# Bias rows by one bf16 matmul, and bent rows completed on VectorE, in a graph attention layer

## The reference

```
q = x @ Wq + bq;  k = x @ Wk + bk;  v = x @ Wv + bv       (8 heads of 16)
e = edge_attr @ We
alpha = sum(q[dst] * (k[src] + e)) / 4        per head
a = exp(alpha - max over dst);  attn = a / sum over dst of a
out = sum over dst of attn * (v[src] + e)
x_r = x @ Wskip + bskip
beta = sigmoid([out, x_r, out - x_r] @ Wbeta);  out = beta * x_r + (1 - beta) * out
out = layernorm(out) * ln_gamma + ln_beta
y = x + relu(out)
result = layernorm(x + y)                      (so the last norm sees 2 x + relu(...))
```

## Time and profile before

| | |
|---|---|
| median of 3 runs | 2780.67 us (2771.22 to 2795.91) |
| profiled execution, span | 2774.7 us |
| PE busy | 2009.6 us (72%), 11492 instructions |
| PEld busy | 1805.8 us (65%) |
| DVE busy | 1801.8 us (65%), 4040 instructions |
| ACT busy | 1140.6 us (41%) |
| POOL busy | 1497.6 us (54%), 1591 instructions |
| mean granted PE clock | 0.770 of full speed |

### The profile page before, as it was taken

How to read it: one execution, slowest core, us unless ns; L and a number is a source line. 1 busy time by engine, 2 the same in 40 slices (tenths; PEclk the granted TensorE clock), 3 DMA queues, 4 the chain that set the end, 5 groups by cost and what they waited for, 6 DMA issues and landing times.

```text
span 2774.7 us, 45026 instructions
## 1 busy us (share of the span) xinstructions
PE 2009.6 (72%) x11492; PEld 1805.8 (65%) x11492; DVE 1801.8 (65%) x4040; ACT 1140.6 (41%) x3750; POOL 1497.6 (54%) x1591
## 2 busy tenths in 40 slices
PE   7478888888776577667766767757687777778775
PEld 5467777777666566566665767656576667667664
DVE  7465565566666566566665667657676676777764
ACT  0133333344343344344443444434454454454455
POOL 0555555555556555565555555555555555555531
PEclk9677777777777777777777777778788777777786
DMA  8556666666655555555554655555565555555541
GB/s 308 185 165 184 176 184 183 178 180 180 172 167 167 158 159 167 154 174 165 167 167 143 176 163 167 175 149 165 164 176 167 170 176 168 169 172 180 169 123 39
DMA packets 298585, 468.47 MB, mean 169 GB/s; under 512 B 49862, under 2 KB 193034, under 8 KB 298230
## 3 DMA queue, kind: packets, MB, share of 16 engines
q1 hardware_dynamic: 222680, 259.30, 31.3%
q0 software_dynamic: 75648, 206.24, 26.2%
HBM read 414.62 MB, written 50.73 MB: 168 GB/s over the span
## 4 chain that ended last, share of the span: by engine, by line
PE 54%; issue 17%; another core or an unknown queue 13%; ACT 8%; DVE 3%; DMA 2%; ACTq 1%; POOL 0%; SPq 0%; POOLq 0%; DVEq 0%
PE sum_ps L928 18%; PE q_ps L825 12%; PE e_ps L812 10%; ACT dist_en L1046 3%; PE max_ps L841 2%; PE sum_ps L866 2%; PE sum_ps L865 2%; PE sum_ps L851 2%; PE max_ps L834 2%; PE sum_ps L850 2%; ACT hot_en L1055 1%; PE sum_ps L894 1%; PE sum_ps L895 1%; DMA xt_buf<-xT 1%
## 5 line engine op out<-in xcount | busy, mean ns | idle before, releaser
L706 POOL DMA_INDIRECT kv<-kv_tab,src_all x1568 | 1483.1, 946 | 1144.6 <-DVE kve L1373 683.8
L1373 DVE TENSOR_TENSOR kve<-kv,e_ps 128x1024 f32<-128x1024 f32 x392 | 462.2, 1218 | 756.0 <-issue 626.2
L928 PE MATMUL sum_ps<-wv,hot_en 128*128 128x136 f32 x3136 | 683.7, 394 | 15.0 <-issue 11.4
L928 PEld LDWEIGHTS sum_ps<-wv,hot_en 128*128 128x128 f32 x3136 | 626.1, 291 | 60.4 <-issue 58.5
L825 PE MATMUL q_ps<-q_win,hot_ne 128*128 128x128 f32 x3136 | 458.8, 284 | 265.2 <-issue 262.8
L825 PEld LDWEIGHTS q_ps<-q_win,hot_ne 128*128 128x128 f32 x3136 | 401.5, 197 | 281.0 <-issue 278.1
L1046 ACT ACTIVATE dist_en<-iota_n,neg_rel 128x128 bf16<-128x128 f32 x1568 | 497.7, 389 | 75.9 <-issue 75.9
L812 PE MATMUL e_ps<-we,ea 128*128 128x128 f32 x3136 | 422.6, 292 | 13.1 <-issue 7.2
L1083 ACT COPY sums<-sum_ps 128x136 f32<-128x136 f32 x392 | 98.3, 263 | 798.5 <-remote 730.6
L812 PEld LDWEIGHTS e_ps<-we,ea 128*128 128x128 f32 x3136 | 415.3, 212 | 12.7 <-issue 6.4
L834 PE MATMUL max_ps<-ident,top 128*1 128x128 f32 x196 | 65.0, 332 | 332.8 <-ACT used_b L1060 296.5
(11 more groups left out here) (136 smaller groups left out, 1573.7 us busy)
## 6 DMA issues: line engine op xcount, KB each, us to landing
ea<-eaT SPq DMA_DIRECT2D x196, 512.0 KB
row_b<-rel_row SPq DMA_DIRECT2D x196, 256.0 KB
kv<-kv_tab,src_all POOLq DMA_INDIRECT x1568
q_win<-q_tab SPq DMA_DIRECT2D x392, 64.0 KB
sum_tab<-sums SPq DMA_DIRECT2D x392, 59.5 KB
kv_tab<-tab_buf SPq DMA_DIRECT2D x33, 384.0 KB, 3.7
logit<-sum_tab SPq DMA_DIRECT2D x49, 136.0 KB
xt_buf<-xT SPq DMA_DIRECT2D x33, 192.0 KB, 4.0
```

What stands on the lines that cost most here:

```text
L706: pool.indirect_dma_start(out=kv[:, s, t, :], out_offset=None, in_=kv_tab[:, :], in_offset=bass.IndirectOffsetOnAxis(ap=src_all[:, tile:ti ...
L928: mm = pe.matmul(sum_ps[u][:, 0:AC], hot_en[:, s, t, :], wv[:, s, t, :], start=(t == 0), stop=(t == TILES_G - 1))
L1373: dve.tensor_tensor(kve[:, s, :, :, :], kv[:, s, :, :].rearrange("p t (a c) -> p t a c", a=2), e4.to_broadcast([P, TILES_G, 2, C]), ALU.ad ...
```

## The change

Three things. The bias rows of `project` and `make_queries` enter by one bf16 matmul over both blocks, ahead of the two f32 matmuls, with K = 3: three rows meant to be three parts of the bias that add up to it. The setup makes them on VectorE. In `turn_back` the four matmuls become two transposes of `u_bent`, and a new stage `lift` on VectorE adds 2 x `u_xt` to `u_bent` first. `back` comes two steps after `bend` instead of in the same step, and all later stages two steps later.

```diff
-STAGES = ("xr", "seen", "gate", "keep", "mix", "inv1", "off1", "unit", "turn", "bend", "back", "rows", "spread", "inv2",
+BIAS_K = 3
+STAGES = ("xr", "seen", "gate", "keep", "mix", "inv1", "off1", "unit", "turn", "bend", "lift", "back", "rows", "spread", "inv2",
           "off2", "norm", "out")
-DELTAS = (0, 1, 0, 1, 0, 1, 0, 1, 1, 1, 0, 1, 0, 1, 0, 1, 1)
+DELTAS = (0, 1, 0, 1, 0, 1, 0, 1, 1, 1, 0, 2, 1, 0, 1, 0, 1, 1)
-STEPS = PAIRS + 20
+STEPS = PAIRS + 22
...
-        ident2 = part(P)
...
+        bias_row = part(CG + C)[0:BIAS_K, :]
+        bias_left = part(CG + C)[0:BIAS_K, :]
+        bias_part = part(BIAS_K, CG + C)[0:BIAS_K, :, :]
+        bias3 = part(2 * P + P)[0:BIAS_K, :].bitcast(BF16)[:, 0:CG + C]
+        ones_b = part(P // 2)[0:BIAS_K, :].bitcast(BF16)
...
-            pe.wait_ge(ident2_ok, 1)
-            pe.wait_ge(bqrow_ok, 1)
+            pe.wait_ge(bias_ok, 7)
...
             def make_queries(r):
                 pe.wait_ge(xq_ld[r % 4], 16 * len(range(r, Q_AHEAD - 1, -4)))
                 n = q_blocks(r)
+                pe.matmul(xr_to[:, 0:n, 0:C], ones_b[:, :], bias3[:, CG:CG + C].unsqueeze(1).to_broadcast([BIAS_K, n, C]),
+                          start=True, stop=False)
                 for b in range(n):
-                    pe.matmul(xr_to[:, b, 0:C], xq[:, r % 4, b:n * P:n], w_kvq[:, 2 * C:3 * C], start=True, stop=False)
-                    mm = pe.matmul(xr_to[:, b, 0:C], ones_f[:, :], bq_row[:, :], start=False, stop=True)
+                    mm = pe.matmul(xr_to[:, b, 0:C], xq[:, r % 4, b:n * P:n], w_kvq[:, 2 * C:3 * C], start=False,
+                                   stop=(b == n - 1))
...
+                pe.matmul(xr_to[0:m, :, :], ones_b[:, 0:m], bias3[:, 0:CG].unsqueeze(1).to_broadcast([BIAS_K, 2, CG]),
+                          start=True, stop=False)
                 for k in range(2):
-                    pe.matmul(xr_to[0:m, k, :], u_xt[:, u % 8, k, 0:m], wskip[:, :], start=True, stop=False)
-                    mm = pe.matmul(xr_to[0:m, k, :], ones_f[:, 0:m], skip_row[:, :], start=False, stop=True)
+                    mm = pe.matmul(xr_to[0:m, k, :], u_xt[:, u % 8, k, 0:m], wskip[:, :], start=False, stop=(k == 1))
...
             def turn_back(u, t):
                 m = height(u)
-                pe.wait_ge(bend_ok, u + 1)
+                pe.wait_ge(lift_ok, u + 1)
...
                 for k in range(2):
-                    pe.matmul(to[0:m, k, :], u_bent[:, u % 3, k, 0:m], ident[:, :], start=True, stop=False)
-                    mm = pe.matmul(to[0:m, k, :], u_xt[:, u % 8, k, 0:m], ident2, start=False, stop=True)
+                    mm = pe.transpose(to[0:m, k, :], u_bent[:, u % 3, k, 0:m], ident[:, :])
...
-            dve.tensor_copy(skip_row[:, 0:C], bskip[0:1, :])
+            dve.tensor_copy(bias_row[:, 0:C], bskip[0:BIAS_K, :])
+            dve.tensor_copy(bias_row[:, CG:CG + C], b_kvq[0:BIAS_K, 2 * C:3 * C]).then_inc(bias_ok, 1)
...
-            dve.tensor_copy(bq_row[:, :], b_kvq[0:1, 2 * C:3 * C]).then_inc(bqrow_ok, 1)
+            dve.memset(ones_b[:, :], 1.0)
             dve.wait_ge(ident_ok, 1)
-            dve.tensor_scalar(ident2, ident[:, :], 2.0, None, ALU.mult).then_inc(ident2_ok, 1)
+            dve.wait_ge(bias_ok, 1)
+            dve.wait_ge(wskip_ok, 2)
+            dve.tensor_copy(bias_part[:, 0, :], bias_row[:, :]).then_inc(bias_ok, 1)
+            dve.wait_ge(bias_ok, 2)
+            dve.tensor_tensor(bias_left[:, :], bias_row[:, :], bias_part[:, 0, :], ALU.subtract).then_inc(bias_ok, 1)
+            dve.wait_ge(bias_ok, 3)
+            dve.tensor_copy(bias_part[:, 1, :], bias_left[:, :]).then_inc(bias_ok, 1)
+            dve.wait_ge(bias_ok, 4)
+            dve.tensor_tensor(bias_part[:, 2, :], bias_left[:, :], bias_part[:, 1, :], ALU.subtract)
+            dve.tensor_scalar(bias3[:, :], bias_part[:, 0, :], ident[0:BIAS_K, 0:1], None, ALU.mult).then_inc(bias_ok, 1)
+            for k in range(1, BIAS_K):
+                dve.wait_ge(bias_ok, 4 + k)
+                dve.scalar_tensor_tensor(bias3[:, :], bias_part[:, k, :], ident[0:BIAS_K, k:k + 1], bias3[:, :], ALU.mult,
+                                         ALU.add).then_inc(bias_ok, 1)
...
+            def lift(u):
+                m = height(u)
+                dve.wait_ge(bend_ok, u + 1)
+                dve.scalar_tensor_tensor(u_bent[:, u % 3, :, 0:m], u_xt[:, u % 8, :, 0:m], 2.0, u_bent[:, u % 3, :, 0:m],
+                                         ALU.mult, ALU.add).then_inc(lift_ok, 1)
...
                 for u in due("gate", t):
                     gate(u)
+                for u in due("lift", t):
+                    lift(u)
                 for u in due("off1", t):
```

33 lines of the change are left out of this document (16 added, 17 removed).

## The result

In the first set the changed kernel took 2849.69 us (median of 5), the kernel before 2771.22 (median of 5). The ratio is 1.026, 95% interval 1.0186 to 1.0337. The range 2748 to 2812 misses it. Later sets gave two things that the first could not show: the same changed kernel at 0.9998, and a kind of chip on which both kernels take 2120 to 2130 us.

A forecast was written before the change was run, and what follows sets the result against it. The prediction took a ring of waits between gathers and `kve`, not TensorE, as the bound. 2774.7 + 2.8 - 3 + 4 - 8 = 2770.5, or 2774 from the before runs' centre; it forecast 2775 us, range 2748 to 2812.

The forecast's parts named there:

- The ring: Main loop: gathers and `kve` wait for each other, 13.1 us a step, TensorE inside the pause; 73% that it holds.
- rival (a): Whole kernel: TensorE is the bound, so most of the 186 us removed go, 2680 us; 4%.
- Early `kve`s: Loop steps where `kve` starts before its usual time: 18 more starts within reach, taken as +4 us, bounds -24 and +45.
- The 3.3 us rule: Steps 4 to 192: `e_ps` under 3.3 us after the first gather gave early `kve` in 18 of 50; later, only step 4.
- Rival (c): Query steps and light steps behind heavy ones: more merged bursts, 7.5 us for each dear pair, 2820 us; 10%.
- The prediction's own sign against itself: Loop: the prediction called itself wrong if more than a few pairs of steps take over 30 us.
- Setup: Before `flag` and the first gathers: added VectorE instructions that split the bias, +2.8 us on the path, bounds 0 and 4.
- rival (e): Bias rows: one bf16 matmul may compile as more or cost as f32; tail +2 us; counted inside the main case.
- rival (d): Gather bursts: each lift on VectorE stops a gather for 0.45 us, +22 us, 2797 us; 4%.
- Inside the ring: Loop steps with `xr` and `back`: removed TensorE work shortens the wait before `kve`, 30 x 0.1 = -3 us, bounds 0 and -5.
- Tail: After the last bursts, TensorE uncovered: fewer matmuls in `project` and `turn_back`, -8 us, bounds 0 and -12.
- The rule of the Trainium skill: Tail: transposes don't count as TensorE activity for the clock; `fix_sums` would take up to 10.4 us, tail -4, not -8.

The follow-up runs named there:

- e15: Changed kernel with the last of each group's four edge tiles left out of the sums, less TensorE work ahead of `e_ps`: 2973.13 us, ratio 1.0714.
- e5: Changed kernel unchanged, run again beside the kernel before on the slower kind of chip: 2781.46 us against 2769.36, ratio 0.9998.
- e6: Kernel before with the edge projection (`e_ps`) moved to the head of TensorE's step, same work: 3230.84 us, ratio 1.1647.
- e1: Kernel before with only the bias rows by bf16 matmul, `turn_back` and its stages as before: 2786.73 us, ratio 0.997.
- e2: Kernel before with only the lift, the transposes and the added delay, bias rows as before: 2794.18 us, ratio 0.9995.
- e3: Changed kernel with TensorE's removed work put back as matmuls whose result is overwritten: 2773.7 us, ratio 0.9968.
- e8: Changed kernel plus one wait: the second group's gathers also wait for both products of the pair two before; 2731.49 us, ratio 0.9853.
- set 2: Second set of runs: both halves, the padding and the exchange, on a slower-kind chip; kernel before 2784.95 us.
- e16: Kernel before plus the gathers' wait for both products of the pair two before, slower kind of chip: 2759.51 us, ratio 0.9929.
- e4: Changed kernel with the spread of the query rows ahead of the edge projection (`e_ps`) in TensorE's order: 2732.46 us, ratio 0.9821.
- e10: Kernel before plus the gathers' wait for both products of the pair two before, faster kind of chip: 2130.79 us, ratio 0.9996.
- e9: Changed kernel unchanged, run again on the faster kind of chip: 2124.61 us, ratio 0.9974.
- e7: Kernel before with only the query spread moved ahead of the edge projection (`e_ps`) in TensorE's order: 2786.24 us, ratio 1.0067.
- e17: Changed kernel unchanged, run again on the faster kind of chip: 2122.1 us, ratio 0.9968.
- e18: Changed kernel with `e_ps` at the head of TensorE's step and the added wait in the gathers' queue, faster kind: 2122.58 us, ratio 0.9974.

## Why the prediction was wrong

**The ring, right for the slower kind of chip.** Its undisturbed steps stay at 12.9 to 13.2 us with TensorE down by 6 to 16 us in ten steps, so rival (a) falls where it was read; e15, slower at 2973 us with the least TensorE work, is the clearest proof. For the faster kind the ring isn't there, and the profile of before could not say so.

**Early `kve`s, the step that failed.** The prediction had 18 more starts of `e_ps` within 3.3 us, 18 of 50 of them early, 1.3 us each: +8, less something for the shorter `project`, +4, with +45 as the bound. In the first set's profile steps 4 to 192 take 2676.9 us against 2504.5, +172; by the medians of the runs some 90 us are left for the term (78 measured, 13 won in the tail). The price of a pair was right (7.5 us predicted, 6.7 measured). What failed is the number of such pairs, in four ways.

- *The share.* The profile has only 5 more starts within reach (55), but 37 of them early, and 11 early ones beyond. The share is not fixed: e5 has 51 and 15, e15 92 and 63, e6 90 and 84. The 3.3 us rule orders the steps of one profile and forecasts none of another.
- *The mean price.* 1.3 us is an average over 11 early ones that cost nothing and 8 that began inside the burst, of which four were dear. In the first set 35 began inside the burst and 31 long steps follow; in e5 11 and 9, in e1, e2 and e3 together 39 and 33. In none of these profiles does a long step follow any other `kve`. The number to forecast was that of the inside ones.
- *The place.* The prediction said that the late steps lose next to nothing. The 36 steps from 157 to 192 take 474.7 us before, with no early `kve`, and 562.7 in the first set's profile, with 14: 88 of the 172 us. No profile of e1, e2, e3, e5 or e8 has more than one early `kve` there. The query steps, from which eight starts were expected, have two.
- *Independence.* In that late stretch each merged pair leads to the next: behind it TensorE has caught up, `e_ps` starts 0 to 2 us after the first gather, and `kve` is early again. Of the steps behind a long one 14 of 31 are early in the first set's profile (ten of them from 175 on), 22 of 35 in e15 and 69 of 76 in e6, but 0 of 4 before, 0 of 9 in e5, and 3 of 33 in e1 to e3. So the count can feed itself and then has no bound of "six more"; in most profiles of the slower kind it does not.

Rival (c) had price and sign right, and its place in part: of the 31 long steps 18 lie in 46 to 156, two in the query steps, 11 behind. Seven more pairs and 10% were too little for a term that all of the change pushes one way. The prediction's own sign against itself, more than a few pairs of steps over 30 us, came in the first set's profile.

**How large the change's own loss is stays open.** Shown are the mechanism and its direction: later `e_ps` 0.982, cut bursts 0.985, more work out 1.071, `e_ps` first 1.165. That the change by itself raises the number of merged bursts is not shown: it gave 1.026 and 0.9998 in two sets on this kind of chip, its halves 0.997 and 0.9995, and with the work put back 0.997. Without the 88 us of the late stretch the first set's profile would stand at 2851 us, among its other four runs; whether these have the stretch isn't known. Why the first set had more merged bursts isn't shown either. Its query steps without an early `kve` are 12.96 us (median), as in set 2, where even the kernel before is slowest, 2785; the profiles of before, e5, e8, e15 and e16 have 13.10 to 13.15. A pause that is shorter by 0.1 us may go with more merging, but no run set it.

**Setup, +2.8 predicted.** `flag` moves from 76.63 to 78.41 us and the first gather from 78.91 to 80.53: +1.6. But this execution began the block 1.0 us earlier. From its first instruction (L1346 before, L1349 changed) to `flag` it takes 1.36 us before and 4.14 changed, +2.8 as worked out, and 4.14 or 4.15 in every other profile that has the new bias rows, 1.2 to 1.4 in those that have not; to the first gather it is 2.6 more. The two `scalar_tensor_tensor` (L1373) take 0.99 us together, where 0.96 was predicted:

```profile
75.27 0.29 DVE L1346 TENSOR_TENSOR w_out<-wbeta 128x128 f32<-128x128 f32 x1
```

```profile
74.27 0.29 DVE L1349 TENSOR_TENSOR w_out<-wbeta 128x128 f32<-128x128 f32 x1
...
77.12 0.34 DVE L1370 TENSOR_SCALAR logit<-logit,ident 3x257 bf16<-3x257 f32 x1
77.50 0.99 DVE L1373 SCALAR_TENSOR_TENSOR logit<-logit,ident 3x257 bf16<-3x257 f32 x2
78.41 0.13 DVE L1376 TENSOR_SCALAR flag<-bad_all 128x1 int32<-128x1 f32 x1
```

**Terms on TensorE.** Groups of the changed kernel:

```profile
L899 PE MATMUL sum_ps<-ident,logit 128*128 128x128 f32 x84 | 25.2, 401 | 0.0
L887 PE MATMUL sum_ps<-ident,logit 128*128 128x128 f32 (+1 forms) x102 | 25.0, 337 | 10.7 <-ACT logit L1115 8.1 <-ACT logit L1107 2.5
L1522 DVE SCALAR_TENSOR_TENSOR logit<-logit 128x256 f32<-128x256 f32 (+1 forms) x51 | 21.2, 416 | 2.1 <-ACT logit L1107 2.1
L868 PE MATMUL sum_ps<-logit 3*128 3x258 bf16 (+1 forms) x51 | 18.7, 366 | 4.9 <-DMA logit<-xT 3.8 <-ACT sums L1086 0.7 <-ACT logit L1093 0.3
```

The bf16 matmul is one instruction of 366 ns (I took 0.3 us), so rival (e) falls; the lift 416 ns (0.45). Two transposes of `turn_back` take 0.65 to 0.68 us on the tail's chain where I took 0.4. The lift costs nothing in the ring (e4 and e8: 13.1 us), and rival (d) falls: with 51 lifts e4's 1568 gathers average 946 ns, as in the earlier trace rows. *Inside the ring*, -3: heavy steps of e16 take 13.32 us (median) and of e8 13.20, so 30 x 0.1, as worked out, though the two ran on different chips.

**Tail, -8 predicted, bounds 0 and -12.** From the start of the last pair's `kve` to the end: 85.7 us before, 73.1 changed; e16 and e8 85.4 and 73.1; on the faster kind e10 and e9 86.0 and 75.2. So -11 to -13, at or past the lower bound. The end, from `fix_sums` on, gave what was worked out (44.53 us before, 41.18 changed: -3.35, predicted -3.2). The part ahead of it gave 9.3 us where 5.4 were predicted. The halves say where: the tail is 80.1 us in e1 and 78.4 in e2, so that the bias half is worth 5.6 (2.2 predicted) and the other 7.3 (6.4).

```profile
2895.27 0.39 PE sum_ps L868
2895.65 1.16 PE sum_ps L871 x4
...
2897.17 0.66 PE e_ps L899 x2
2897.83 6.64 PE q_ps L981 x32
```

The rule of the Trainium skill ("TensorE: Matmul & The Clock Gate", Part 4: PE-mode transpose) would have made `fix_sums` up to 10.4 us. It took 6.64 at a mean granted clock of 0.66, against 6.07 at 0.86, so a little of that came. But e1, with four f32 matmuls in `turn_back` and no transposes there, has 6.58; e2, with the transposes and the f32 bias rows, 6.68; and e3, with the transposes and the work put back, 5.88. Either half of the change gives the longer time, so the transposes are not needed for it. Whether they count for the clock no run here isolates, since e3 adds matmuls and takes no transpose away.

```profile
2897.80:2904.50 6.70, 6.70 (x34) 6.57 (x32) 2.38 (x13) 3.11 (x11) 0.00 (x0) 0.66 0.07 21
```

On the faster kind, where nothing merges at a price, the sum is what the prediction's small terms say: -11 for the tail, +2 for the setup, and +2 in steps 4 to 193, -7 together, against -7.1 between the profiles of e9 and e10 (2123.1 and 2130.2 us).

## What to carry to other kernels

Where a ring of waits sets the pace, look for what happens when one member is early, not only when it is late: here an early `kve` buys up to 5 us and costs up to 13 in the step behind it, and less work made it more frequent (e15). When a rare exception is priced, count apart the cases that cost and those that don't: a mean over both forecasts neither. If a few places of a profile show a costly exception, ask whether the state that they leave behind makes the next one likely; then take as the bound the kernel in which all steps are such, which a one-line reordering (e6) can measure. Cutting the long burst by one wait that is met anyway (e8), or running what needn't be early later (e4), gave, together with the change, 1.5 and 1.8% on the slower kind of chip, where the change alone won nothing. In the kernel before the wait gave 0.7% (e16) and the later order lost 0.7% (e7). A version that wins on one kind should be run on the other: the gate was, in the kernel before, with no loss; the exchange was not.

## What the runs showed of the hardware

- Chips, or their states, differ. On three the kernel before takes 2128 to 2130 us, on three known others 2769 to 2785, 30% more, with equal times of gathers and of `kve` (946 to 949 ns, 1.22 us) and a mean granted clock of 0.91 against 0.77. What differs is how waits pass while GpSimd issues gathers one behind the other. On the slower kind most stand until 1.8 to 2.9 us after the last of 8 to 16 gathers; not all do, since the second `kve` of the merged pair shown above starts at 2679.34, amid the 16. On the faster kind ScalarE's `used_b` copies wait 48.5 us in all. No run shows why.
- On the slower kind a wait of GpSimd in the middle of a burst ends the standstill of the others (e8, 2.3 us after the last gather).
- On the faster kind the same time was measured at two granted clocks: e17 has a mean of 0.93 and takes 2122.1 us, e18 on the same chip 0.85 and 2122.6. On the slower kind it is 0.75 in steps 46 to 155 of the changed kernel and 0.70 in the alternating stretch, where TensorE is busy 76.9 of 169.8 us; in e9's steps 46 to 156, with the same work in less time, it is 0.93.
- A bf16 matmul of 3 rows and 258 columns, one pass, takes 366 ns; one of the two records of an f32 matmul over 129 columns takes 437 (L871 of the same page).
